# A graph network on one core: 16 of 2048 gathered rows of each body move from POOL's gather to single-row transfers of SP, empty edge tiles are skipped, and the setup is ordered anew

## The chip, the cores and the metric

One Trainium2 chip, one core. The metric is the device time of one launch in microseconds (us), the median of several runs. Less is better.

## The reference

Two graph-network layers over 6250 nodes with 160 features and 200,000 edges that are sorted by destination. Cut to what matters:

```
for layer in (0, 1):
    h   = node_features @ W_in * attr                 # a table of 6250 rows of 160 floats (640 B)
    w   = silu(edge_inputs @ fc1) @ fc2               # weights of each edge
    msg = w * h[edge_src] * edge_attr                 # one table row is gathered for each edge
    agg = segment_sum(msg, edge_dst)                  # summed at the destination nodes
    node_features = f(node_features, agg @ W_out, attr)   # layer norm with a residual between and after
```

The source nodes are random, so the rows `h[edge_src]` are read one by one from a table in HBM.

## The kernel before

There are five phases, with a barrier between them: `setup_phase` (weights, the first table, a table of destination windows), `edge_phase` for layer 0, `layer0_nodes_phase` (node update and the second table), `edge_phase` for layer 1, and `layer1_nodes_phase`.

The edges are padded to 200,704 and cut in tiles of 128 (one edge on each partition). Four tiles make a group, four groups a body, and there are 98 bodies. In `edge_phase` each engine runs its own loop over the bodies:

- POOL issues one indirect gather for each tile (`gather`, L542): 128 rows of 640 B from the table to `rows[j]`, by the tile's column of indices. A group's gathers wait until the sums that read the same buffer in the body before are done (`sum_done`), and until the index tile has come (`index_in`).
- SP loads, for each half body, the next indices (L484), the edge inputs (L489) and the edge attributes (L493); in the first 50 bodies also a node tile (L500 and L501 in layer 0, L503 and L507 in layer 1). The index load of a half waits until the gathers that used the buffer have landed (L483). Its two loops, over pairs of bodies, stand at L517 and L522.
- TensorE makes the hidden layer (L587), the edge weights (L600) and the products with one-hot matches that sum the messages by destination (L607). For each group it first loads a value from SBUF into a register (L644) and then waits (L647).
- ScalarE applies silu and scales the matches (L571).
- VectorE multiplies weights with gathered rows (L800 to L808, behind a wait on `gathered[j]`) and adds the sums. It loads a value for each group too (L707).

The order of the work is written out by hand, and all waits are on semaphores. Semaphores of a DMA rise by 16 when it has landed.

Of the kernel before, what the change touches and what calls it, by code (L numbers as in the profile page):

```python
# [11 lines left out]
P = 128  # L12
# [15 lines left out]
TPG = 4  # L28
# [22 lines left out]
INDEX_BUFFERS = 4  # L51
assert BODIES % 2 == 0 and NT % 2 == 0 and INDEX_BUFFERS == 4
# [54 lines left out]
def setup_phase(nc, d, w, sums):  # L107
    with ExitStack() as ctx:
# [37 lines left out]
        low, grp, totalled, counted = (sem(n) for n in ("low", "grp", "totalled", "counted"))  # L146
# [23 lines left out]
        def _(sp):  # L170
# [17 lines left out]
            for name in OTHERS:  # L188
                sp.dma_start(w[name][:, :], d[name]).then_inc(weights_in, 16)
            sp.dma_start(dst_tile[:, :], d["dst_tile"]).then_inc(dtile_in, 16)  # L190
# [4 lines left out]
            for c in range(len(STORES) - 1):  # L195
                store(c)
                if STORES[c + 1] == 30:
                    sp.wait_ge(low, 2)
                    sp.dma_start(d["lo_dram"].rearrange("(p q) -> p q", q=GQ), lo_i[:, :]).then_inc(lo_out, 16)
                if STORES[c + 1] == 40:  # L200
                    sp.wait_ge(lo_out, 16)
                    sp.dma_start(lo_all[:, :], d["lo_dram"].rearrange("(a g) -> a g", a=1).broadcast_to([P, G])).then_inc(lo_in, 16)
                    sp.wait_ge(grp, 12)
# [72 lines left out]
        def _(pe):  # L276
# [34 lines left out]
            for k in range(NT):  # L311
                project(k)
                if k == 35:
                    count_extras()
                if k == 41:
                    centre()
# [4 lines left out]
        def _(dve):  # L321
# [10 lines left out]
            def lowest():  # L332
                dve.wait_ge(dst_in, 16)
                nc.vector.tensor_reduce(lo_f[:, :], dst_by_group[:, :, :], mybir.AxisListType.X, ALU.min).then_inc(low, 1)

            def lowest_kept():
                dve.wait_ge(low, 1)
                nc.vector.tensor_scalar(lo_i[:, :], lo_f[:, :], float(NPAD - 1), None, ALU.min).then_inc(low, 1)

            def highest():  # L340
                nc.vector.tensor_reduce(hi_f[:, :], dst_by_group[:, :, :], mybir.AxisListType.X, ALU.max).then_inc(grp, 1)

            def spans():
                dve.wait_ge(grp, 1)
                nc.vector.scalar_tensor_tensor(out=span_f[:, :], in0=hi_f[:, :], scalar=float(NPAD - 1), in1=lo_f[:, :],
                                               op0=ALU.min, op1=ALU.subtract).then_inc(grp, 1)
                dve.wait_ge(grp, 2)
                nc.vector.tensor_scalar(span_i[:, :], span_f[:, :], 0.0, None, ALU.max).then_inc(grp, 1)

            def extras():  # L350
                dve.wait_ge(grp, 3)
                nc.vector.tensor_scalar(span_i[:, :], span_i[:, :], 3, None, ALU.arith_shift_right).then_inc(grp, 1)
                dve.wait_ge(grp, 4)
                nc.vector.tensor_scalar(span_i[:, :], span_i[:, :], 205, None, ALU.mult).then_inc(grp, 1)
                dve.wait_ge(grp, 5)
                nc.vector.tensor_scalar(entries[:, :, 1], span_i[:, :], 10, None, ALU.arith_shift_right).then_inc(grp, 1)

            def totals():
                dve.wait_ge(grp, 6)
                nc.vector.tensor_copy(extra_f[:, :], entries[:, :, 1]).then_inc(grp, 1)  # L360
                dve.wait_ge(low, 2)
                nc.vector.scalar_tensor_tensor(out=entries[:, :, 0], in0=lo_i[:, :], scalar=float(1 << EXTRA_BITS),
                                               in1=entries[:, :, 1], op0=ALU.mult, op1=ALU.add)
                dve.wait_ge(grp, 7)
# [4 lines left out]
            def partial(q):  # L369
                dve.wait_ge(grp, 8 + q)  # L370
                nc.vector.tensor_tensor(part_sum[:, q + 1:q + 2], part_sum[:, q:q + 1], extra_f[:, q:q + 1], ALU.add).then_inc(grp, 1)

            def table_entries():
                dve.wait_ge(grp, 11)
# [20 lines left out]
            for k in range(NT):  # L395
# [3 lines left out]
                if k == 13:  # L399
                    lowest()  # L400
                if k == 17:
                    highest()
                if k == 25:
                    lowest_kept()
                if k == 27:
                    spans()
                if k == 29:
                    extras()
                if k == 31:
                    totals()  # L410
                if k in (33, 34, 35):
                    partial(k - 33)
                if k == 38:
                    table_entries()
                if k == 45:
# [5 lines left out]
            relative()  # L421
# [3 lines left out]
def edge_phase(nc, d, w, sums, nodes, layer):  # L425
# [3 lines left out]
    with ExitStack() as ctx:  # L429
# [32 lines left out]
        prepared, zeroed = sem("prepared"), sem("zeroed")  # L462
# [8 lines left out]
        sum_done, added = sem("sum_done"), sem("added")  # L471
        x_rel, x_tile, x_matched, x_sum_done, x_added = (sem(n) for n in ("x_rel", "x_tile", "x_matched", "x_sum_done", "x_added"))
# [5 lines left out]
        def _(sp):  # L478
            def load(i, q, k):
                later = not (isinstance(i, int) and i == 0)  # L480
                if later:
                    for j in (2 * q, 2 * q + 1):
                        sp.wait_ge(gathered[j], GATHERED * i)  # L483
# [24 lines left out]
            def body(i, parity, with_base):  # L508
                for q in range(2):
                    load(i, q, (2 * parity + q + 2) % INDEX_BUFFERS)  # L510
                if with_base:
                    load_base(i)
                if with_base and L == 1 and not (isinstance(i, int) and i == 0):
                    store_self(i - 1)
# [757 lines left out]
```

## Time and profile before

| | |
|---|---|
| median of 3 runs | 4147.22 us (4146.08 to 4151.31) |
| profiled execution, own time | 4158.72 us |
| its span | 4157.0 us |
| POOL busy | 3019.7 us (73%) |
| PE (TensorE matmul) busy | 3299.3 us (79%) |
| ACT (ScalarE) busy | 2898.8 us (70%) |
| DVE (VectorE) busy | 2369.4 us (57%) |
| granted TensorE clock, mean | 0.988 |

The busy share is an average over the phases. SP issues DMAs and runs register instructions only; none of these count as busy, so the table has no row for it. An engine's sequencer, which runs such instructions, is written with a q (SPq, DVEq, PEldq).

### The profile page before, as it was taken

The page shows a single profiled execution, that of the slowest core. Times are in us where ns is not written, and L with a number is a line of the kernel's source. Part 1 is how long each engine was busy: PE and PEld are TensorE (multiplying, and loading weights), DVE is VectorE, ACT ScalarE, POOL GpSimd, SP SyncE. Part 2 cuts the span into 40 slices and gives each one's busy share as a digit, 9 for nine tenths or more (in the row PEclk, how much of TensorE's full clock was granted, in tenths as well). Part 3 has the DMA queues.
Part 4 walks back from the last instruction along what each step waited for, and adds up shares of the span by engine and source line. Part 5 has one row for each costly group of instructions (what it writes and reads, how often), then busy time and mean ns, then how long its engine had stood idle before and what let it go on. Part 6 is the DMA issues. An engine that isn't in the chain of part 4 may idle for free. (4 is left out here: it accounts for less than half of the span.)

```text
span 4157.0 us, 230556 instructions
## 1 busy us (share of the span) xinstructions
PE 3299.3 (79%) x91130; PEld 2543.6 (61%) x91131; DVE 2369.4 (57%) x6461; ACT 2898.8 (70%) x12105; POOL 3019.7 (73%) x3206
## 2 busy tenths in 40 slices
PE   7788888888777777777888888888878777777776
PEld 6666666666555555555766666666656565655656
DVE  5555555555444444444556666666666666666666
ACT  6666666666666666666477777777778777777776
POOL 5777777777777777777457777777777777777771
PEclk9999999999999999999999999999999999999998
DMA  5333333333222222222243434434333333333333
GB/s 154 83 83 82 85 82 83 82 82 85 73 72 73 72 73 72 72 73 72 77 131 105 107 104 107 107 104 107 104 105 98 93 94 96 93 96 94 93 96 107
DMA packets 361825, 382.01 MB, mean 92 GB/s; under 512 B 173617, under 2 KB 282997, under 8 KB 361662
## 3 DMA queue, kind: packets, MB, share of 16 engines
q0 software_dynamic: 150528, 257.10, 24.2%
q1 hardware_dynamic: 209936, 122.14, 10.4%
q10 hardware_dynamic: 1296, 1.91, 0.2%
q8 instruction: 39, 0.64, 0.1%
q14 instruction: 26, 0.21, 0.0%
HBM read 357.10 MB, written 23.76 MB: 92 GB/s over the span
## 5 line engine op out<-in xcount | busy, mean ns | idle before, releaser
L542 POOL DMA_INDIRECT e_rows<-scratch_table,k_index x3136 | 2972.7, 948 | 997.4 <-issue 900.6
L571 ACT ACTIVATE e_match<-e_match,e_attr 128x40 f32<-128x40 f32 x10976 | 2476.7, 316 | 0.0
L607 PE MATMUL e_sum<-e_match,e_msg 128*32 128x40 f32 (+1 forms) x81536 | 1438.0, 215 | 707.1 <-DVE e_msg L805 362.5
L607 PEld LDWEIGHTS e_sum<-e_match,e_msg 128*32 128x32 f32 x81536 | 1294.1, 111 | 1024.4 <-DVE e_msg L808 396.7
L800 DVE TENSOR_TENSOR e_msg<-e_w,e_rows 128x512 f32<-128x512 f32 x784 | 542.2, 692 | 1681.8 <-DMA e_rows<-scratch_table,k_index 1643.4
L564 ACT ACTIVATE e_hidden<-e_h 100x512 f32<-100x512 f32 (+1 forms) x784 | 384.7, 491 | 1138.0 <-PE e_h L587 1134.7
L600 PE MATMUL e_w<-k_fc,e_hidden 100*128 100x192 f32 (+1 forms) x6272 | 1025.5, 365 | 1.0 <-issue 1.0
L600 PEld LDWEIGHTS e_w<-k_fc,e_hidden 100*128 100x128 f32 (+1 forms) x6272 | 807.2, 189 | 348.1 <-issue 330.4
L587 PE MATMUL e_h<-e_inputs,k_fc 128*100 128x512 f32 (+1 forms) x1568 | 708.7, 534 | 116.6 <-issue 59.3
L803 DVE TENSOR_TENSOR e_msg<-e_w,e_rows 128x384 f32<-128x384 f32 x784 | 429.0, 547 | 0.0
L805 DVE TENSOR_TENSOR e_msg<-e_w,e_rows 128x384 f32<-128x384 f32 x784 | 429.0, 547 | 0.0
L587 PEld LDWEIGHTS e_h<-e_inputs,k_fc 128*100 128x100 f32 (+1 forms) x1568 | 216.7, 177 | 200.5 <-issue 152.0
L702 DVE TENSOR_TENSOR e_match<-e_misc,k_dst_rel 128x160 f32<-128x160 f32 x788 | 248.8, 316 | 2.1 <-issue 0.7
L736 DVE TENSOR_TENSOR sums<-sums,e_sum 128x160 f32 x784 | 242.9, 310 | 9.3 <-PE e_sum L607 8.5
L807 DVE TENSOR_TENSOR e_msg<-e_w,e_rows 128x384 f32<-128x384 f32 x392 | 214.2, 547 | 0.0
L808 DVE TENSOR_TENSOR e_msg<-e_w,e_rows 128x384 f32<-128x384 f32 x392 | 213.9, 546 | 0.0
L791 DVE TENSOR_TENSOR e_match<-e_misc,e_match 128x160 f32<-128x160 f32 x392 | 123.6, 315 | 0.0
L779 DVE COPY e_e_kept<-e_attr 128x48 f32<-128x48 f32 x392 | 81.7, 209 | 6.5 <-issue 3.6
L865 POOL MEMSET sums<- 128x512 f32 (+1 forms) x50 | 26.4, 528 | 59.1 <-PE m_agg L937 59.1
L903 ACT ACTIVATE m_yT<-m_tr 128x256 f32<-128x256 f32 x50 | 19.2, 386 | 47.9 <-PE m_tr L944 47.9
L778 DVE COPY e_misc<-e_attr 128x48 f32<-128x48 f32 x196 | 40.5, 207 | 10.3 <-DMA e_attr<-in_edge_attr 1.2
L1066 ACT ACTIVATE f_post<-f_pre 128x64 f32<-128x64 f32 x50 | 12.4, 248 | 31.4 <-DVE f_pre L1100 31.4
(130 smaller groups left out, 1032.7 us busy)
## 6 DMA issues: line engine op xcount, KB each, us to landing
e_rows<-scratch_table,k_index POOLq DMA_INDIRECT x3136
e_inputs<-in_inputs SPq DMA_DIRECT2D x196, 256.0 KB
e_attr<-in_edge_attr SPq DMA_DIRECT2D x392, 24.0 KB
e_inputs<-in_inputs SPq DMA_DIRECT2D x196, 40.0 KB
e_xb<-in_xT SPq DMA_DIRECT2D x50, 128.0 KB
scratch_yT<-m_yT SPq DMA_DIRECT2D x10, 640.0 KB, 4.6
e_xb<-scratch_yT SPq DMA_DIRECT2D x50, 128.0 KB
k_index<-in_src SPq DMA_DIRECT2D x396, 4.0 KB, 5.4
```

The source lines that it names most:

```text
L542: pool.indirect_dma_start(out=rows[j][:, t, :], out_offset=None, in_=table_dram, in_offset=bass.IndirectOffsetOnAxis(ap=index[k][:, c:c + ...
L564: nc.scalar.activation(hidden[j % 2][:, :], ps_h[0:layer.hid, 0:layer.group_cols], ACT.Silu, scale=layer.silu_scale).then_inc(silu_done, 1)
L571: last = nc.scalar.activation(match[j][:, t, c, :], match[j][:, t, 4, :], ACT.Copy, scale=attr[q][:, e0 + t, e:e + 1])
L587: nc.tensor.matmul(ps_h[0:layer.hid, 0:n], w[f"fc1_{L}"][:, :], inputs[j // 2][:, (j % 2) * n:(j % 2) * n + n], start=True, stop=True).the ...
L600: last = nc.tensor.matmul(ps_w[j % 2][:, c0:c0 + n], hidden[j % 2][k * h:k * h + k, u * P:(u + 1) * P], fc2[k * h:k * h + k, :], start=Tru ...
L607: return nc.tensor.matmul(out[32 * g:32 * g + 32, c0:c0 + n, :], m[:, f:f + 32], m5[:, which:which + n, :], start=first and opens, stop=en ...
L702: return nc.vector.tensor_tensor(into[:, :, 4, :], iota_t, rel_of(g).unsqueeze(2).broadcast_to([P, TPG, WIN]), ALU.is_equal)
L736: nc.vector.tensor_tensor(at, at, window, ALU.add).then_inc(added, 1)
L800: nc.vector.tensor_tensor(m[:, :, 0:128].rearrange("p t (k n) -> p t k n", k=2), wt[:, :, 0:128].rearrange("p t (k n) -> p t k n", k=2), r ...
L803: nc.vector.tensor_tensor(comps(m[:, :, 128:224]), w_v(128), comps(r[:, :, 64:160]), ALU.mult)
L805: last = nc.vector.tensor_tensor(comps(m[:, :, 224:320]), w_v(160), comps(r[:, :, 64:160]), ALU.mult)
L807: nc.vector.tensor_tensor(comps(m[:, :, 320:416]), w_v(192), comps(r[:, :, 64:160]), ALU.mult)
```

## The change

It has three parts.

1. The last tile of each body (group 3, tile 3) is gathered by POOL for partitions 0 to 111 only. SP fetches rows 112 to 127: for each it loads the index from SBUF into a register and issues a DMA of one row from the table into `sp_rows` (one of two buffers). Eight rows are fetched behind the first half's loads and eight at the body's end. In the next body, behind the first half's loads, SP copies the 16 rows with one DMA into the group's tile. VectorE's multiplies of group 3 wait for that copy too (`sp_copied`).
2. The padding, which stood at the end of the edge list, is now the first tiles of the first body: `EMPTY = (2, 1, 1, 1)` tiles of its four groups. They are cleared by VectorE and not gathered (five gathers fewer in each phase); waits on `gathered` change by as much.
3. The setup has another order: reductions of the destination table are made in four parts each and later, the first store of the table stands ahead of other loads, and `relative()`, which makes the relative destinations, stands at tile 41 where it stood at the end.

```diff
+EMPTY = (2, 1, 1, 1)
+BY_SP = 16
+BY_POOL = P - BY_SP
...
+            def copy_rows(i, parity):
+                landed, summed = 16 * BY_SP * i + 16 * BY_SP, GPB * i
+                if not isinstance(i, int):
+                    sp.compute_val(landed)
+                    sp.compute_val(summed)
+                sp.wait_ge(sp_landed, landed)
+                at_least(sp, sum_done, summed)
+                sp.dma_start(rows[GPB - 1][BY_POOL:P, TPG - 1, :], sp_rows[parity][BY_POOL:P, :]).then_inc(sp_copied, 16)
+
+            def fetch_rows(pair, parity, first, last):
+                i, k = 2 * pair + parity, 2 * parity + 1
+                if first == BY_POOL:
+                    if not isinstance(pair, int):
+                        used, copied = 32 * pair, 16 * i - 16
+                        sp.compute_val(used)
+                        sp.compute_val(copied)
+                        sp.wait_ge(prepared, 1)
+                        sp.wait_ge(index_in[k], used)
+                        sp.wait_ge(sp_copied, copied)
+                for p in range(first, last):
+                    row = sp.value_load(index[k][p:p + 1, STEP - 1:STEP], min_val=0, max_val=NPAD - 1)
+                    sp.dma_start(sp_rows[parity][p:p + 1, :], table_dram[bass.ds(row, 1), :]).then_inc(sp_landed, 16)
+
+            def body(pair, parity, with_base):
+                i, half = 2 * pair + parity, BY_POOL + BY_SP // 2
+                started = not (isinstance(i, int) and i == 0)
+                load(i, 0, (2 * parity + 2) % INDEX_BUFFERS)
+                if started:
+                    copy_rows(i - 1, 1 - parity)
+                fetch_rows(pair, parity, BY_POOL, half)
+                load(i, 1, (2 * parity + 3) % INDEX_BUFFERS)
+                if with_base:
+                    load_base(i)
+                if with_base and L == 1 and started:
+                    store_self(i - 1)
+                fetch_rows(pair, parity, half, P)
...
+                first = isinstance(count, int) and not parity
...
-                for t in range(TPG):
+                for t in range(EMPTY[j] if first else 0, TPG):
                     c = (j % 2) * TPG + t
+                    p = BY_POOL if (j, t) == (GPB - 1, TPG - 1) else P
                     pool.indirect_dma_start(
-                        out=rows[j][:, t, :], out_offset=None, in_=table_dram,
-                        in_offset=bass.IndirectOffsetOnAxis(ap=index[k][:, c:c + 1], axis=0),
+                        out=rows[j][0:p, t, :], out_offset=None, in_=table_dram,
+                        in_offset=bass.IndirectOffsetOnAxis(ap=index[k][0:p, c:c + 1], axis=0),
                     ).then_inc(gathered[j], 16)
...
-                dve.wait_ge(gathered[j], GATHERED * i + GATHERED)
+                dve.wait_ge(gathered[j], GATHERED * i + GATHERED - 16 * EMPTY[j])
+                if j == GPB - 1:
+                    dve.wait_ge(sp_copied, 16 * i + 16)
...
-                if k == 13:
-                    lowest()
-                if k == 17:
-                    highest()
+                if k in (24, 25, 26, 27):
+                    lowest(k - 24)
+                if k in (28, 29, 30, 31):
+                    highest(k - 28)
...
+                if k == 41:
+                    relative()
...
-            relative()
             dve.wait_ge(rel_made, 2)
```

SP's queue in layer 0's second loop, one body without node tile, before. `ISA` is a register instruction; L484, L489 and L493 are the three loads of a half body.

```order
L484 ISA
L484 DMA k_index<-in_src 128x8
L485 ISA
L489 ISA
L489 DMA e_inputs<-in_inputs 10x1024
L491 REGISTER_ALU
L493 ISA
L493 DMA e_attr<-in_edge_attr 128x48
L484 ISA
L484 DMA k_index<-in_src 128x8
L489 ISA
L489 DMA e_inputs<-in_inputs 10x1024
```

The same place now, from the attribute load of the first half on (L506 is what L493 was). L528 is the copy of the 16 rows of the body before, L535 the head of `fetch_rows`, and L541 and L542 are a row's value load and its address and DMA.

```order
L506 DMA e_attr<-in_edge_attr 128x48
L524 ISA
L528 DMA e_rows<-e_sp_rows 16x160
L535 ISA
L541 TENSOR_LOAD k_index
L541 ISA x2
L542 ISA
L542 DMA e_sp_rows<-scratch_table 1x160
L541 TENSOR_LOAD k_index
L541 ISA x2
L542 ISA
L542 DMA e_sp_rows<-scratch_table 1x160
```

The four rows from L541 on stand eight times there, and eight times more behind the second half's loads.

## Rows read from the trace of the kernel before

**Rows 1.** The page's costliest groups: busy, mean ns of one, idle before with releasers.

```profile
L542 POOL DMA_INDIRECT e_rows<-scratch_table,k_index x3136 | 2972.7, 948 | 997.4 <-issue 900.6
...
L800 DVE TENSOR_TENSOR e_msg<-e_w,e_rows 128x512 f32<-128x512 f32 x784 | 542.2, 692 | 1681.8 <-DMA e_rows<-scratch_table,k_index 1643.4
```

**Rows 2.** POOL's timeline, one body of layer 0: start us, duration us.

```profile
1000.00 0.95 POOL L542 DMA_INDIRECT e_rows<-scratch_table,k_index  x1 [0.30 <-issue]
1001.25 0.94 POOL L542 DMA_INDIRECT e_rows<-scratch_table,k_index  x1 [0.30 <-issue]
...
1020.04 0.95 POOL L542 DMA_INDIRECT e_rows<-scratch_table,k_index  x1 [0.30 <-issue]
```

**Rows 3.** POOL's waits over the whole span: us in total, times, longest.

```profile
POOL e_rows L542 <- PE e_sum L607: 55.1, 181, 0.3
```

**Rows 4.** SP's timeline, a body without node tile: start us, duration us.

```profile
1987.45 0.35 SPq L484 DMA_DIRECT2D k_index<-in_src  x1
...
1988.72 0.34 SPq L493 DMA_DIRECT2D e_attr<-in_edge_attr  x1
...
1998.03 0.30 SPq L489 DMA_DIRECT2D e_inputs<-in_inputs  x1
1998.57 0.34 SPq L493 DMA_DIRECT2D e_attr<-in_edge_attr  x1
```

**Rows 5.** SP's line L483 in two short windows: ns min/median/max, first and last start.

```profile
L483 SPq EVENT_SEMAPHORE  x1: 17/17/17, 1987.2 to 1987.2; - x1
...
L483 SPq EVENT_SEMAPHORE  x1: 17/17/17, 1997.3 to 1997.3; - x1
```

**Rows 6.** SP's timeline, second half of a body with node tile.

```profile
1016.32 0.35 SPq L493 DMA_DIRECT2D e_attr<-in_edge_attr  x1
1016.90 0.35 SPq L500 DMA_DIRECT2D nodes<-in_x  x1
1017.45 0.33 SPq L501 DMA_DIRECT2D e_xb<-in_xT  x1
```

**Rows 7.** Line L517, the end of SP's loop over pairs.

```profile
L517 SPq FUSED_REGOPS  x48: 50/50/60, 76.1 to 3059.1; - x48
L517 SPq ALU_OP  x48: 37/37/37, 115.9 to 3098.9; - x48
L517 SPq COMPARE_BRANCH  x48: 40/45/59, 115.9 to 3099.0; - x48
```

**Rows 8.** TensorE's value load L644 and the instruction behind it, window 1003.5 to 1004.6.

```profile
L644 PEldq FUSED_REGOPS  x2: 55/103/151, 1003.7 to 1004.2; - x2
L644 PEldq TENSOR_LOAD <-k_table x1: 302/302/302, 1003.8 to 1003.8; - x1
L644 PEldq SEQ_ASSERT  x1: 18/18/18, 1004.4 to 1004.4; - x1
...
L647 PEldq EVENT_SEMAPHORE  x1: 51/51/51, 1004.5 to 1004.5; - x1
```

**Rows 9.** Value loads of TensorE (L644) and VectorE (L707), all of them.

```profile
L644 PEldq TENSOR_LOAD <-k_table x784: 296/300/488, 61.0 to 4083.6; - x196
...
L707 DVEq TENSOR_LOAD <-k_table x784: 302/306/552, 64.4 to 4083.2; - x196
```

**Rows 10.** Line L501: SP's register instructions ahead of a DMA with a computed address.

```profile
L501 SPq FUSED_REGOPS  x48: 42/43/43, 95.4 to 1037.4; - x48
L501 SPq MOVE e_xb<-in_xT x48: 29/29/29, 95.4 to 1037.5; - x48
```

**Rows 11.** Line L207: SP's one DMA that has a single partition (1x1568).

```profile
L207 SPq DMA_DIRECT2D k_table<-scratch_tab_dram x1: 242/242/242, 47.4 to 47.4; - x1
```

**Rows 12.** Timeline, end of setup and start of layer 0's edge phase.

```profile
48.02 1.78 DVE L387 SCALAR_TENSOR_TENSOR k_dst_rel<-dst_tile_i,lo_all 128x1568 f32<-128x1568 int32 x1
...
51.49 1.10 POOL L542 DMA_INDIRECT e_rows<-scratch_table,k_index  x1 [30.05 <-POOLq L108]
...
62.23 0.69 DVE L800 TENSOR_TENSOR e_msg<-e_w,e_rows 128x512 f32<-128x512 f32 x1 [6.22 <-PE e_w L600]
```

**Rows 13.** SP's waits over the whole span.

```profile
SPq L211 <- DMA scratch_table<-h: 1.1, 1, 1.1
```

**Rows 14.** Timeline: the first attribute load, and VectorE released by it.

```profile
53.39 0.36 SPq L493 DMA_DIRECT2D e_attr<-in_edge_attr  x1
...
55.25 0.21 DVE L778 COPY e_misc<-e_attr 128x48 f32<-128x48 f32 x1 [1.21 <-DMA e_attr<-in_edge_attr]
```

More of the change, by code:

```diff
@@ L51 @@
 INDEX_BUFFERS = 4
+EMPTY = (2, 1, 1, 1)
+BY_SP = 16
+BY_POOL = P - BY_SP
+assert 0 <= EPAD - EDGES - sum(EMPTY) * P <= (TPG - EMPTY[0]) * P
 assert BODIES % 2 == 0 and NT % 2 == 0 and INDEX_BUFFERS == 4
@@ L189, in _ @@
                 sp.dma_start(w[name][:, :], d[name]).then_inc(weights_in, 16)
+            store(0)
             sp.dma_start(dst_tile[:, :], d["dst_tile"]).then_inc(dtile_in, 16)
@@ L471, in edge_phase @@
         sum_done, added = sem("sum_done"), sem("added")
+        sp_rows = [sb(f"sp_rows{b}", [P, D]) for b in range(2)]
+        sp_landed, sp_copied = sem("sp_landed"), sem("sp_copied")
         x_rel, x_tile, x_matched, x_sum_done, x_added = (sem(n) for n in ("x_rel", "x_tile", "x_matched", "x_sum_done", "x_added"))
@@ L481, in load @@
                 if later:
+                    landed = [GATHERED * i - 16 * EMPTY[j] for j in (2 * q, 2 * q + 1)]
+                    if not isinstance(i, int):
+                        for value in landed:
+                            sp.compute_val(value)
                     for j in (2 * q, 2 * q + 1):
-                        sp.wait_ge(gathered[j], GATHERED * i)
+                        sp.wait_ge(gathered[j], landed[j - 2 * q])
                     sp.dma_start(index[k][:, :], d["src"][:, bass.ds((2 * i + q + 2) * STEP, STEP)]).then_inc(index_in[k], 32)
@@ L507, in store_self @@
                 sp.dma_start(d["self1"][bass.ds(i * P, P), :], self_t[:, :]).then_inc(self_out, 16)
-            def body(i, parity, with_base):
-                for q in range(2):
-                    load(i, q, (2 * parity + q + 2) % INDEX_BUFFERS)
+            def copy_rows(i, parity):
+                landed, summed = 16 * BY_SP * i + 16 * BY_SP, GPB * i
+                if not isinstance(i, int):
+                    sp.compute_val(landed)
[3 more added lines that the diff above has]
+                sp.dma_start(rows[GPB - 1][BY_POOL:P, TPG - 1, :], sp_rows[parity][BY_POOL:P, :]).then_inc(sp_copied, 16)
@@ L523, in _ @@
                 for parity in range(2):
-                    body(2 * pair + parity, parity, False)
+                    body(pair, parity, False)
+            copy_rows(BODIES - 1, 1)
             for k in range(2):
@@ L810, in messages @@
                 return window_at
+            for j in range(GPB):
+                nc.vector.memset(rows[j][:, 0:EMPTY[j], :], 0.0).then_inc(cleared, 1)
             for g in range(AHEAD):
@@ L1215, in lay_out, with in_slots @@
     r["attr"] = by_partition(padded(np.concatenate([a["node_vec1"], a["node_vec1_n2"], a["node_vec1_n3"]], 1), NPAD))
-    r["src"] = by_partition(padded(a["src"], EPAD + 2 * STEP * P))
-    dst = padded(a["dst"], EPAD, NODES)
+    slot = np.full(EPAD, -1)
+    free = np.ones(EPAD, bool)
+    for g in range(GPB):
+        free[g * GE:g * GE + EMPTY[g] * P] = False
+    free[EMPTY[0] * P:EPAD - EDGES - sum(EMPTY[1:]) * P] = False
+    slot[free] = np.arange(EDGES)
+    following = np.minimum.accumulate(np.where(slot < 0, EDGES, slot)[::-1])[::-1]
+    def in_slots(v):
+        return np.where((slot >= 0).reshape((-1,) + (1,) * (v.ndim - 1)), v[following], 0).astype(v.dtype)
+    r["src"] = by_partition(padded(in_slots(a["src"]), EPAD + 2 * STEP * P))
+    dst = a["dst"][following]
     r["dst_tile"] = by_partition(dst)
     r["dst_by_group"] = dst.reshape(GP, GQ, GE)
-    e = padded(a["edge_attr_4"], EPAD)
+    e = in_slots(a["edge_attr_4"])
     r["edge_attr"] = by_partition(np.concatenate([e, e[:, 1:3]], 1))
-    r["inputs0"] = padded(a["edge_attr_10"], EPAD).T.copy()
-    r["inputs1"] = padded(a["edge_attr_64"], EPAD).reshape(G, 2, 2, P, NB1).transpose(1, 4, 0, 2, 3).reshape(2 * NB1, EPAD // 2)
+    r["inputs0"] = in_slots(a["edge_attr_10"]).T.copy()
+    r["inputs1"] = in_slots(a["edge_attr_64"]).reshape(G, 2, 2, P, NB1).transpose(1, 4, 0, 2, 3).reshape(2 * NB1, EPAD // 2)
     L0 = {k[7:]: v for k, v in a.items() if k.startswith("L0_gnn_")}
```

70 lines of the change are left out of this document (36 added, 34 removed).

## The prediction

> **What bounds the kernel now.** I read the page's costliest groups first, since they give each engine's busy time with what ended its idle time [rows 1]: POOL issues 3136 gathers, busy 2972.7 us, and its idle time of 997.4 us is nearly all "issue", a gap that belongs to the instruction. VectorE's first multiply of a group (L800) is idle 1681.8 us before it, 1643.4 of them for the gathered rows. So rows are what is late, and POOL makes them. POOL's timeline shows how regular that is [rows 2]: 16 gathers, one body, from 1000.00 to 1020.04, so 20.04 us a body and 1.2525 us a gather (0.95 busy, 0.30 gap). The waits of POOL [rows 3] show that TensorE's sums, which free the row buffers, cost it 55.1 us over 181 times, 0.30 each: the same gap, not a wait. Both edge phases have 98 bodies, 196 x 20.04 = 3928 us of a span of 4157.0.
>
> Then SP, which is to get new work. It has nothing busy in the page, but its timeline shows its queue [rows 4, 5]. In a body without node tile it passes the first wait (L483) at 1987.2 and ends its third DMA at 1989.06; it passes the second at 1997.3 and ends at 1998.91. That is 1.86 + 1.61 us of work, with 8.2 us of waiting between. The two loads of a node tile (bodies 0 to 49 of each phase) add 1.1 us: the DMA before them starts at 1016.32 and ends at 1016.67, the last ends at 1017.78 [rows 6]. The loop's end costs some 0.3 us for two bodies (three short instructions of 37 to 50 ns and their gaps) [rows 7]. SP thus works 3.6 or 4.7 us of 20.04; some 15 to 16 us are free. The change asks for them.
>
> **The change: 16 rows a body on SP.** Each row is a value load (a load, a fused register instruction, an assert), an address instruction and a DMA of one row, as the order shows. No SP value load is in the trace, but TensorE's has the same three instructions: load starts at 1003.8, assert at 1004.4, the next instruction (L647) at 1004.5 [rows 8], so 0.6 to 0.7 us, of which the load records 0.30 and the fused instruction 0.15. VectorE's loads take 0.306, so this duration hardly depends on the engine [rows 9]. SP's gaps between short instructions are smaller than TensorE's (its wait instruction takes 17 ns [rows 5] and TensorE's 51 [rows 8]); I take 0.61. From below it is 0.30 + 0.15 + 0.02 and three gaps of 0.03: 0.56; from above 0.67, TensorE's own. The address: between the DMA of L500 (1016.90 + 0.35) and that of L501 (1017.45) lie 0.20 us, which hold a fused instruction of 43 ns, a move of 29 ns and gaps [rows 6, 10]; I take 0.19. The DMA itself: the one transfer with a single partition took SP 0.242 us [rows 11], against 0.30 to 0.35 of the wider ones [rows 4]; I take 0.24, bounds 0.22 and 0.30. Sum: 0.61 + 0.19 + 0.24 = 1.04 us a row (bounds 0.97 and 1.10), and 16.6 us for 16 rows.
>
> **The copy and the waits.** The copy of 16 rows into the group's tile is one more DMA of 0.35 us, a register instruction and two waits with gaps: 0.5. The head of the row fetch (one register instruction, three waits): 0.2. In the other loads the new wait values go into register instructions that are there already: 0.
>
> **SP's body.** Without node tile 1.86 + 1.66 (with the gap behind) + 0.15 + 0.5 + 0.2 + 16.6 = 21.0 us; with it 22.1 us. Both are over POOL's 20.04. SP then never waits, and it is the bound, because every loop closes through it: POOL's index tiles, TensorE's inputs and the attributes are its loads, and VectorE's last group of each body now also waits for its copy. Behind a row fetch stand, in SP's queue, the second half's loads; they come 8.3 us later in the body, still within a period. The other loops are shorter than 21 us: from the sum that frees a row buffer to the next sum of the same buffer it is four gathers (5.0), landing, multiplies and products, some 13 us. Per phase 48 bodies lose 21.0 - 20.04 = 0.96 and 50 lose 2.06, in both phases 92 + 206 = 298 us.
>
> **The other parts.** Five gathers fewer in each phase are 10 x 1.2525 = 12.5 us of POOL. They move POOL ahead at a phase's start only; with SP as the bound they are worth 0. The gather of 112 rows: the trace has only 128. Between 0 (all fixed) and an eighth of 0.95, 0.12 us, less; here hidden under SP, 0 again. The clears of the five tiles (VectorE) lie in its wait of 6.22 us before the first L800 [rows 12]. Setup: taking the 1.78 us instruction L387 from VectorE's end to k = 41 frees little, since the release waits for the last table store: SP's wait at L211 is 1.1 us, and VectorE had ended at 49.80 with POOL's first gather at 51.49 [rows 12, 13]. In its new place it delays the last stores by what VectorE can't absorb. Splitting the reductions moves work, it adds some small gaps. I take 0, bounds -3 and +3.
>
> **The sum.** Profiled execution 4158.7 + 298 = 4457; the median of the three times is 4147.2, 11.5 lower, so 4445 us, 7.2% over before.
>
> **Rivals.**
> 1. *SP keeps up, POOL stays the bound: faster.* It needs a row at 0.90 us or less (5.5 + 14.4 = 19.9). For it: SP's short instructions are quicker than TensorE's, and the row DMA has no equal in the trace. Against: load, fused instruction and DMA alone record 0.30 + 0.15 + 0.24 = 0.69; assert, address and move (0.09) and six gaps then have 0.21, so 0.02 a gap, where SP's three between L500 and L501 have (0.20 - 0.07) / 3 = 0.04 each. Gain: 12.5 for the empty tiles, up to 196 x 0.12 = 23 for the narrower gather: 4112 (4108 to 4135). Chance 0.14. It decides at about 0.92 us a row over all bodies: there what the bodies with node tile lose is what the others win.
> 2. *SP binds mostly in the bodies with node tile.* A row at 0.93 to 0.97: 4165 to 4290. Chance 0.09.
> 3. *The copy waits for its rows.* Between the last row's issue and the copy's wait lie about 0.3 + 1.9 = 2.2 us; the first attribute load, issued at 53.39, had released VectorE at 55.25, 1.86 us later [rows 14]. Landings 1 us later would cost 196 x 0.8 = 157 us: about 4600, and more if they queue. The Trainium skill, "DMA: Bandwidth & Descriptors", section "Why a DMA increments its semaphore by 16 and not by 1", has one-partition transfers from SP all on the one lowest engine; the trace names no engines, so nothing here shows it, and it would speak for this rival. Chance 0.06.
> 4. *The load itself is twice as long on SP.* Records of 0.60 for 0.30 give 1.34 a row, bodies of 25.8 and 26.9, and 557 + 690 = 1247 us: 5394. Against it are TensorE's and VectorE's nearly equal 0.30. The Trainium skill, same page, section "Latency and other measured facts", gives a load to a register a floor of about 600 ns; the rows have 0.30 for the instruction and 0.6 from its start to its assert, so the trace agrees only if the figure means the latter. Chance 0.03.
>
> **How the numbers follow.** My forecast has 0.68: with the row at 0.98 to 1.10, 4300 to 4630. The range leaves out rival 1 (0.14) and rival 4 with the worst of rival 3 (0.05), and reaches from rival 2's start to a row at 1.10 with a copy that waits 0.5: 4160 to 4690. A measurement of this kernel tells about 0.2% (8 us). Faster 0.14, same 0.03, slower 0.83.
>
> **What would show it.** Right: SP has hardly a wait left in the edge phases; POOL's gaps grow and are released by sums or by the index load; L800's wait for the last group of a body is for the copy; bodies of about 21 and 22 us, the first half of a phase slower than the second. A row's pitch on SP is read between two of its DMAs (1.04). Wrong: SP still waits for gathered rows each half body, and POOL's pitch is unbroken. That happens if SP's value load is much under 0.6 us. The 112-row gather shows its own duration either way.

## The result and the profile after

| | before | this kernel |
|---|---|---|
| median (6 runs each) | 4147.18 us | 5303.53 us |
| lowest to highest | 4146.08 to 4151.31 | 5274.97 to 5310.06 |
| profiled execution, own time / span | 4158.72 / 4157.0 | 5276.04 / 5274.3 |
| granted TensorE clock, mean | 0.988 | 0.842 |

The ratio over all runs is 1.2769 (1.2751 to 1.2787; the two medians alone give 1.2788): 28% slower. The forecast was 4445 us. The direction came out as forecast, and so did the bound, SP; the size didn't: SP costs 5.8 us a body over POOL's 20.04, where 1.5 was forecast.

Page of the kernel after: its first line, two lines of the 40 slices (POOL's digit is its busy time in tenths of a slice, and it is 5 or 6 nearly everywhere, so the loss is spread over both edge phases; PEclk is the granted TensorE clock in tenths of full speed), and four of the costliest groups, with idle time and its releaser, which answer to [rows 1].

```profile
span 5274.3 us, 250541 instructions
...
POOL 5555555555565565656445555555555656565652
PEclk8888888888888888888988888888888888888878
...
L587 POOL DMA_INDIRECT e_rows<-scratch_table,k_index x3126 | 2953.5, 945 | 2127.0 <-PE e_sum L652 1253.0
...
L632 PE MATMUL e_h<-e_inputs,k_fc 128*100 128x512 f32 (+1 forms) x1568 | 868.5, 642 | 1404.9 <-DMA e_inputs<-in_inputs 1390.2
L849 DVE TENSOR_TENSOR e_msg<-e_w,e_rows 128x512 f32<-128x512 f32 x784 | 542.0, 691 | 2334.3 <-PE e_w L645 2324.1
L609 ACT ACTIVATE e_hidden<-e_h 100x512 f32<-100x512 f32 (+1 forms) x784 | 384.1, 490 | 2277.1 <-PE e_h L632 2273.2
```

Read it backwards from POOL. The gathers take as long as before, but 2127.0 us of idle time stand ahead of them instead of 997.4, most of it for TensorE's sums. The multiply L849 (L800 before) no longer waits for gathered rows but for edge weights (L645), and the first matmul of the hidden layer (L632) waits for `e_inputs`, a load of SP. TensorE ties the two together: its program order is the hidden layer of a group, the edge weights of the group before, and the sums of the group before that, so that all three stand behind one load. The timeline shows it once (start us, duration us; in brackets the idle time before and what ended it).

```profile
1303.13 1.14 PE L632 MATMUL e_h<-e_inputs,k_fc 128*100 128x512 f32 x2 [3.94 <-DMA e_inputs<-in_inputs]
...
1304.06 2.77 PE L645 MATMUL e_w<-k_fc,e_hidden 100*128 100x192 f32 x8
...
1304.30 0.60 ACT L609 ACTIVATE e_hidden<-e_h 100x512 f32<-100x512 f32 x1 [4.53 <-PE e_h L632]
...
1306.76 1.62 PE L652 MATMUL e_sum<-e_match,e_msg 128*32 128x120 f32 x80
1306.93 0.69 DVE L849 TENSOR_TENSOR e_msg<-e_w,e_rows 128x512 f32<-128x512 f32 x1 [6.14 <-PE e_w L645]
...
1309.26 0.95 POOL L587 DMA_INDIRECT e_rows<-scratch_table,k_index  x1 [3.36 <-PE e_sum L652]
```

The weights at 1304.06 start before ScalarE's activation at 1304.30, and the sums at 1306.76 before the multiply at 1306.93: what held both was TensorE's own order, not the data of this group. The gather at 1309.26 follows the sums.

SP's waits, before and after (us in total, times, longest). Before:

```profile
SPq L483 <- DMA e_rows<-scratch_table,k_index: 1638.5, 209, 9.5
```

After; L528 is the copy's wait:

```profile
SPq L497 <- DMA e_rows<-scratch_table,k_index: 3.1, 12, 0.7
...
SPq L528 <- DMA e_sp_rows<-scratch_table: 1.4, 2, 0.7
```

SP has hardly a wait left in the edge phases, so it is the bound. Its timeline shows the second half of a body with node tile and the first half of the next (start us, duration us; a row with x8 runs from the start of the first to the end of the last):

```profile
1301.02 0.29 SPq L502 DMA_DIRECT2D e_inputs<-in_inputs  x1
1301.56 0.36 SPq L506 DMA_DIRECT2D e_attr<-in_edge_attr  x1
...
1304.02 9.08 SPq L542 DMA_DIRECT2D e_sp_rows<-scratch_table  x8
1313.87 0.39 SPq L497 DMA_DIRECT2D k_index<-in_src  x1
...
1315.17 0.36 SPq L506 DMA_DIRECT2D e_attr<-in_edge_attr  x1
1315.73 0.55 SPq L528 DMA_DIRECT2D e_rows<-e_sp_rows  x1
1317.53 9.06 SPq L542 DMA_DIRECT2D e_sp_rows<-scratch_table  x8
```

Eight rows hold seven pitches: (9.08 - 0.26) / 7 = 1.26 us a row, where 1.04 was forecast and 1.10 was the upper bound. Copies follow one another at 26.4 us where there is a node tile and at 25.2 without one, in both layers (forecast 22.1 and 21.0). 100 bodies lose 6.3 us and 96 lose 5.2, together 1129; with the 4147 of before that is 5276, the time of the profiled execution. (Four of the six runs took 27 to 34 us more than that one; their mean granted clock was 0.835 or 0.836, that of the other two 0.842 and 0.839. None of the four has a profile, and their surplus stays open.)

SP's lines of one row (ns min/median/max, first and last start):

```profile
L541 SPq TENSOR_LOAD <-k_index x3136: 467/499/736, 52.1 to 5194.2; - x196
L541 SPq FUSED_REGOPS  x3136: 152/152/192, 52.6 to 5194.8; - x196
L541 SPq SEQ_ASSERT  x3136: 18/18/33, 52.8 to 5195.0; - x196
...
L542 SPq FUSED_REGOPS  x3136: 37/37/48, 52.9 to 5195.0; - x196
L542 SPq MOVE e_sp_rows<-scratch_table x3136: 29/38/125, 53.0 to 5195.1; - x196
L542 SPq DMA_DIRECT2D e_sp_rows<-scratch_table x3136: 154/260/310, 53.1 to 5195.2; - x196
```

The medians sum to 1.00 us, so 0.25 is gaps, as assumed. One record stands out: the load takes 0.50, not the 0.30 that it takes on TensorE and VectorE [rows 9].

### The profile page after: what moved, and what is told of

Same layout as the page of the kernel before. It is cut to its first block and busy times, and to the rows that moved or that the text cites. A ratio compares the mean times of both kernels' runs of the same rounds, so it can differ in the third digit from the quotient of the medians.

```text
span 5274.3 us, 250541 instructions
## 1 busy us (share of the span) xinstructions
PE 3834.3 (73%) x91130; PEld 2944.9 (56%) x91131; DVE 2492.1 (47%) x6475; ACT 2897.4 (55%) x12105; POOL 3000.5 (57%) x3196
## 5 line engine op out<-in xcount | busy, mean ns | idle before, releaser
L587 POOL DMA_INDIRECT e_rows<-scratch_table,k_index x3126 | 2953.5, 945 | 2127.0 <-PE e_sum L652 1253.0
L632 PE MATMUL e_h<-e_inputs,k_fc 128*100 128x512 f32 (+1 forms) x1568 | 868.5, 642 | 1404.9 <-DMA e_inputs<-in_inputs 1390.2
L849 DVE TENSOR_TENSOR e_msg<-e_w,e_rows 128x512 f32<-128x512 f32 x784 | 542.0, 691 | 2334.3 <-PE e_w L645 2324.1
L652 PEld LDWEIGHTS e_sum<-e_match,e_msg 128*32 128x32 f32 x81536 | 1427.8, 122 | 325.6 <-issue 300.4
L652 PE MATMUL e_sum<-e_match,e_msg 128*32 128x40 f32 (+1 forms) x81536 | 1550.3, 230 | 4.3 <-issue 3.5
L645 PE MATMUL e_w<-k_fc,e_hidden 100*128 100x192 f32 (+1 forms) x6272 | 1343.0, 453 | 0.5 <-issue 0.5
L645 PEld LDWEIGHTS e_w<-k_fc,e_hidden 100*128 100x128 f32 (+1 forms) x6272 | 1045.3, 239 | 467.9 <-issue 431.3
L632 PEld LDWEIGHTS e_h<-e_inputs,k_fc 128*100 128x100 f32 (+1 forms) x1568 | 252.4, 205 | 1495.3 <-issue 1456.5
L916 POOL MEMSET sums<- 128x512 f32 (+1 forms) x50 | 26.4, 527 | 60.7 <-PE m_agg L988 60.7
L1017 DVE SCALAR_TENSOR_TENSOR nodes<-m_agg,k_masked,nodes 128x160 f32<-128x160 f32 x50 | 19.2, 384 | 23.8 <-PE m_agg L988 23.0
```

Source lines behind the costliest of these rows:

```text
L587: pool.indirect_dma_start(out=rows[j][0:p, t, :], out_offset=None, in_=table_dram, in_offset=bass.IndirectOffsetOnAxis(ap=index[k][0:p, c: ...
L632: nc.tensor.matmul(ps_h[0:layer.hid, 0:n], w[f"fc1_{L}"][:, :], inputs[j // 2][:, (j % 2) * n:(j % 2) * n + n], start=True, stop=True).the ...
L645: last = nc.tensor.matmul(ps_w[j % 2][:, c0:c0 + n], hidden[j % 2][k * h:k * h + k, u * P:(u + 1) * P], fc2[k * h:k * h + k, :], start=Tru ...
L652: return nc.tensor.matmul(out[32 * g:32 * g + 32, c0:c0 + n, :], m[:, f:f + 32], m5[:, which:which + n, :], start=first and opens, stop=en ...
L849: nc.vector.tensor_tensor(m[:, :, 0:128].rearrange("p t (k n) -> p t k n", k=2), wt[:, :, 0:128].rearrange("p t (k n) -> p t k n", k=2), r ...
```

## The experiments

In all, the time is device time, each run is one kernel that was executed 2 to 11 times, the ratio is to the kernel before on the same chip (medians 4147.5, 4148.3 and 4149.5 in the three batches). Diffs are against this kernel unless said otherwise.

### First batch: the parts without SP's rows

**e1_rest.** Empty tiles and new setup alone; POOL gathers all 128 rows and SP fetches none.

```diff
                 load(i, 0, (2 * parity + 2) % INDEX_BUFFERS)
-                if started:
-                    copy_rows(i - 1, 1 - parity)
-                fetch_rows(pair, parity, BY_POOL, half)
                 load(i, 1, (2 * parity + 3) % INDEX_BUFFERS)
...
-                fetch_rows(pair, parity, half, P)
...
-                    p = BY_POOL if (j, t) == (GPB - 1, TPG - 1) else P
+                    p = P
...
-                if j == GPB - 1:
-                    dve.wait_ge(sp_copied, 16 * i + 16)
```

> The changed kernel without its first part: POOL gathers all 128 rows of the last tile and SP fetches none, so that only the empty tiles and the new setup are left. Theory A (all of the loss is SP's row work, the rest is harmless): ten gathers fewer at 1.2525 us are 12.5 us, and in the changed kernel's trace POOL's first gather starts at 49.8 instead of 51.5 us, 1.7 us; so about 14 us under before, near 4133 us. Rival B (something in the rest costs too, such as VectorE's extra waits in every group or the moved padding): at or over 4147 us.

Measured: 4139.72 us (4135.18 to 4141.80), ratio 0.9981 (0.9972 to 0.9990): 7.8 us gained where 14 were expected. So all of the loss belongs to the change's first part, the 16 rows, and the rest is a small gain.

**e2_empty.** The kernel before with the empty tiles alone: e1_rest with the old `setup_phase`.

```diff
-                for t in range(TPG):
+                for t in range(EMPTY[j] if first else 0, TPG):
```

> Before with the empty tiles alone, its own setup kept. Theory A: POOL is the bound and starts five gathers ahead in each phase, 12.5 us, near 4134.7 us. Rival: the head start is given back, because in the second body POOL waits for the first body's sums, which the first edge weights hold back anyway: then near 4147, and the gain of the full rest is the setup's.

Measured: 4140.24 us, ratio 0.9979 (0.9970 to 0.9988), so 7.3 us gained where ten gathers make 12.5. POOL's timeline at the start of both phases, and its waits, show where the missing 5 can have gone:

```profile
66.28 0.94 POOL L579 DMA_INDIRECT e_rows<-scratch_table,k_index  x1 [0.69 <-PE e_sum L644]
...
76.53 0.95 POOL L579 DMA_INDIRECT e_rows<-scratch_table,k_index  x1 [0.55 <-PE e_sum L644]
...
2152.38 0.94 POOL L579 DMA_INDIRECT e_rows<-scratch_table,k_index  x1 [3.12 <-PE e_sum L644]
...
POOL e_rows L579 <- PE e_sum L644: 97.7, 298, 3.1
```

At 0.30 a gap, 298 gaps are 89.4 us; 8.3 are real waits, where before it was 55.1 - 181 x 0.30 = 0.8 [rows 3]. POOL comes earlier to buffers that TensorE still reads. That is 7.5 us more, even somewhat over the missing 5; it comes from two single profiles, and the rest stays open.

**e3_setup.** The kernel before with the new `setup_phase` alone.

```diff
-                if k == 13:
-                    lowest()
-                if k == 17:
-                    highest()
+                if k in (24, 25, 26, 27):
+                    lowest(k - 24)
+                if k in (28, 29, 30, 31):
+                    highest(k - 28)
...
+                if k == 41:
+                    relative()
...
-            relative()
```

> Before with the new setup alone. Theory A: the first gather starts 1.7 us earlier, near 4145.5 us. My prediction had 0 with bounds of 3 us on both sides. Rival: within 0.5 us of before, the 1.7 us being chance of one profile.

Measured: 4147.84 us, ratio 1.0000 (0.9991 to 1.0009). In the single profiles the first gather starts at 49.83 instead of 51.49 us, but the times don't show it: within 0.5 us of before, as the rival had it.

**e4_pool112.** e1_rest, with POOL's gather of 112 rows in the last tile. Rows 112 to 127 of that buffer are filled once a phase, with rows that the reference doesn't take.

```diff
+            sp.dma_start(rows[GPB - 1][112:P, TPG - 1, :], table_dram[0:P - 112, :]).then_inc(filled, 16)
...
                 if isinstance(i, int):
                     dve.wait_ge(cleared, GPB)
+                    dve.wait_ge(filled, 16)
```

> As the first kernel of this call (empty tiles and new setup), but POOL gathers only 112 rows in the last tile of each body. Rows 112 to 127 of that tile are left out: they are filled once a phase with the table's first rows, and SP fetches nothing after that. Theory A: a gather's cost is nearly fixed; single gathers of 112 rows in the changed kernel's trace take 0.93 us against 0.94 to 0.95, so 196 x 0.015 is 3 us under the first kernel of this call. Rival C, the upper bound of my prediction: an eighth of 0.95, 196 x 0.12 is 23 us under it.

Measured: 4139.38 us, ratio 0.9979 (0.9970 to 0.9988), as e1_rest. Two gathers in a row, the second with 112 rows:

```profile
1001.59 0.94 POOL L583 DMA_INDIRECT e_rows<-scratch_table,k_index  x1 [0.30 <-issue]
1002.84 0.92 POOL L583 DMA_INDIRECT e_rows<-scratch_table,k_index  x1 [0.30 <-issue]
```

An eighth fewer rows makes a gather 0.02 us shorter, not 0.12: its cost is nearly all fixed. 196 x 0.02 = 4 us at most, and that doesn't show. The 23 us of the rival don't exist. What SP took over was worth nothing to POOL.

### Second batch: why a row takes 1.26 us

Open was why the load takes 0.50: a load on SP is slow in itself (S), it is slow behind a transfer (Q), or it depends on the partition it reads from, 112 and up (P).

**s1_loads.** Sixteen loads a body stay, the sixteen transfers go; one transfer of the last row to all 16 partitions takes their place, so 15 rows are not those of the reference.

```diff
-                landed, summed = 16 * BY_SP * i + 16 * BY_SP, GPB * i
+                landed, summed = 16 * i + 16, GPB * i
...
-                    sp.dma_start(sp_rows[parity][p:p + 1, :], table_dram[bass.ds(row, 1), :]).then_inc(sp_landed, 16)
+                if first != BY_POOL:
+                    sp.dma_start(sp_rows[parity][BY_POOL:P, :], table_dram[bass.ds(row, 1), :].broadcast_to([BY_SP, D])).then_inc(sp_landed, 16)
```

> The changed kernel with its 16 value loads a body, but without their 16 row transfers: one transfer a body brings 16 copies of one row, so the other 15 rows of the tile are left out. In the changed kernel a row takes SP 1.25 us, of it 0.50 for the load's own record, where TensorE's and VectorE's loads take 0.30. Theory S (a load simply takes SP 0.50): loads still record 0.50, 0.80 us from load to load, SP has about 19.5 us of work a body with node tile and POOL is the bound again or nearly so, 4135 to 4180 us. Theory Q (a load waits for the transfer that SP issued just ahead of it): behind another load it records 0.30, 0.60 from load to load, and SP waits 3 us a body more.

Measured: 4139.00 us, ratio 0.9977 (0.9966 to 0.9989). The load's line over the whole span, and then over one block of eight:

```profile
L541 SPq TENSOR_LOAD <-k_index x3136: 267/274/749, 51.2 to 4046.7; - x196
...
L541 SPq TENSOR_LOAD <-k_index x8: 274/275/473, 1306.3 to 1310.4; - x8
```

A load takes 0.27 us, except one of each eight, with 0.47 here: the first, which has the attribute load's DMA ahead of it. In the body's other block of eight the first stands behind the copy, with the head of `fetch_rows` between, and takes 0.56. Sixteen loads still fit under POOL.

**s2_transfers.** The sixteen transfers stay, from constant rows; the loads go.

```diff
-                    row = sp.value_load(index[k][p:p + 1, STEP - 1:STEP], min_val=0, max_val=NPAD - 1)
-                    sp.dma_start(sp_rows[parity][p:p + 1, :], table_dram[bass.ds(row, 1), :]).then_inc(sp_landed, 16)
+                    sp.dma_start(sp_rows[parity][p:p + 1, :], table_dram[p:p + 1, :]).then_inc(sp_landed, 16)
```

> The changed kernel with the 16 row transfers but without the value loads: the rows' addresses are constants, so the rows brought are not the edge's. Both theories: 0.26 us and a gap, 0.31 us a row, 5 us a body, SP at about 11 us of 20; POOL is the bound, near 4140 us as the rest alone. If instead the transfers or their landing were the cost (my third rival: they queue, the copy waits for them), it stays well over 4200 us.

Measured: 4139.42 us, ratio 0.9979 (0.9968 to 0.9991). A line and a stretch of the timeline:

```profile
L541 SPq DMA_DIRECT2D e_sp_rows<-scratch_table x3136: 162/252/438, 52.3 to 4043.1; - x196
...
1318.61 2.36 SPq L541 DMA_DIRECT2D e_sp_rows<-scratch_table  x8
```

That is (2.36 - 0.25) / 7 = 0.30 us a transfer. Neither half of a row's work alone is slow, and neither alone takes SP over POOL's 20.04 us a body, the threshold from which SP is the bound.

**s3_grouped.** All of the work, with the eight loads ahead of the eight transfers.

```diff
-                for p in range(first, last):
-                    row = sp.value_load(index[k][p:p + 1, STEP - 1:STEP], min_val=0, max_val=NPAD - 1)
+                loaded = [sp.value_load(index[k][p:p + 1, STEP - 1:STEP], min_val=0, max_val=NPAD - 1) for p in range(first, last)]
+                for p, row in zip(range(first, last), loaded):
                     sp.dma_start(sp_rows[parity][p:p + 1, :], table_dram[bass.ds(row, 1), :]).then_inc(sp_landed, 16)
```

> The changed kernel with eight value loads first and their eight transfers after, the work being the same. Theory S: loads record 0.50, a body stays at 26.4 us, 5300 us within 30. Theory Q: seven of eight loads record 0.30, a body is 16 x 0.875 x 0.2 = 2.8 us shorter, near 4750 us.

Measured: 4489.39 us (4488.45 to 4490.33), ratio 1.0823 (1.0792 to 1.0855): 814 us less for another order of the same instructions. Lines and timeline:

```profile
L540 SPq TENSOR_LOAD <-k_index x3136: 267/274/726, 52.4 to 4402.9; - x196
...
L540 SPq TENSOR_LOAD <-k_index x8: 273/274/469, 1302.3 to 1306.4; - x8
...
L542 SPq DMA_DIRECT2D e_sp_rows<-scratch_table x3136: 207/228/315, 57.3 to 4406.6; - x196
...
1307.11 3.14 SPq L542 DMA_DIRECT2D e_sp_rows<-scratch_table  x8
```

The loads are at 0.27 again. Of the seven pitches in 4.1 us the first is 0.20 longer, so the others are (4.1 - 0.2) / 7 = 0.56; a transfer with its address is (3.14 - 0.23) / 7 = 0.42. With an eighth of those 0.20 a row is then 1.0 us, where it was 1.26; copies follow one another at 22.35 and 21.15 us, 4.1 less than in this kernel. S falls: the same load on the same engine is at 0.27. Q gave the direction, but the run is some 260 us better than the 4750 that Q expected: the loads account for 3.1 us of the 4.1 (14 of them 0.225 shorter), the shorter transfers (0.228 for 0.260) for 0.5, and the gaps for the rest. Why those shrank is open.

**s4_partition0.** The loads read partitions 0 to 15 (other rows than the reference's).

```diff
-                    row = sp.value_load(index[k][p:p + 1, STEP - 1:STEP], min_val=0, max_val=NPAD - 1)
+                    row = sp.value_load(index[k][p - BY_POOL:p - BY_POOL + 1, STEP - 1:STEP], min_val=0, max_val=NPAD - 1)
```

> The changed kernel, but SP's loads read the indices of partitions 0 to 15 instead of 112 to 127 (so it fetches other edges' rows). TensorE's and VectorE's loads of 0.30 read partition 0. Theory P (the partition matters): loads record 0.30, a body is 3.2 us shorter, near 4680 us. Theories S and Q: 0.50 and 5300 us within 30.

Measured: 5253.01 us, ratio 1.2664 (1.2627 to 1.2701).

```profile
L541 SPq TENSOR_LOAD <-k_index x3136: 458/493/721, 50.9 to 5171.7; - x196
```

The load stays at 0.49. P, which expected 4680, falls. The two executions are 17 us under the range of S and Q; loads that are 0.006 us shorter make 19 of the 24 us between the two profiled executions, and the rest stays open.

So the load is slow behind a transfer and quick behind another load. On SP no run has a load with neither just ahead of it, so "behind a transfer" and "not behind a load" aren't told apart there; TensorE's and VectorE's loads at 0.30 [rows 9] come once a group, with neither ahead, but on other engines.

### Third batch: the threshold

SP's body is 16 rows plus 5.07 us (6.26 with a node tile); it crosses POOL's 20.04 at a row of 0.94 (0.86). Four kernels go from the row of 1.26 towards and under that.

**f2_nocheck.** Loads still behind transfers, without the range check of each index (a fused instruction of 0.15 and an assert).

```diff
-                    row = sp.value_load(index[k][p:p + 1, STEP - 1:STEP], min_val=0, max_val=NPAD - 1)
+                    row = nc.s_assert_within(sp.value_load(index[k][p:p + 1, STEP - 1:STEP]), 0, NPAD - 1,
+                                             skip_runtime_bounds_check_because="indices are below NPAD")
```

> The changed kernel without the range check of the value loads, each load still right behind a transfer. Theory T with loads that stay at 0.50 behind a transfer: 1.256 - 0.25 is 1.00 us a row, bodies of 22.3 and 21.2 us, 4150 + 100 x 2.25 + 96 x 1.1 is about 4480 us. Rival: without the check's instructions the load's latency shows in the address instruction instead and the row stays at 1.1 us or more: 4630 us or over.

Measured: 4390.28 us, ratio 1.0583 (1.0562 to 1.0604).

```profile
L541 SPq TENSOR_LOAD <-k_index x3136: 441/504/727, 51.3 to 4309.5; - x196
...
L543 SPq DMA_DIRECT2D e_sp_rows<-scratch_table x3136: 254/263/305, 52.0 to 4310.2; - x196
...
1317.41 7.14 SPq L543 DMA_DIRECT2D e_sp_rows<-scratch_table  x8
```

A row is (7.14 - 0.26) / 7 = 0.98, so the check costs 0.27, more than its two records (0.17). Copies follow one another at 21.85 and 20.65 us, where 22.3 and 21.2 were expected, so the run is 90 us under the 4480 of theory T; the rival's 4630 falls. The load stays at 0.50: the check, which stood between the load and the row's own transfer, isn't what makes it slow.

**f1_grouped_nocheck.** s3_grouped and f2_nocheck in one, all parts of the change and the whole computation.

```diff
+                loaded = [nc.s_assert_within(sp.value_load(index[k][p:p + 1, STEP - 1:STEP]), 0, NPAD - 1,
+                                             skip_runtime_bounds_check_because="indices are below NPAD")
+                          for p in range(first, last)]
+                for p, row in zip(range(first, last), loaded):
```

> All three parts of the change kept, 16 rows on SP, but eight value loads stand together ahead of their eight transfers, and the loads have no range check (a fused instruction and an assert, 0.25 us with gaps). Theory T (SP's work per body against POOL's 20.04 us decides, and nothing else of the change costs): the row falls from 1.00 us (grouped) to 0.75, SP's body with node tile from 22.3 to 18.3 us, SP waits for POOL again, and the time is that of the rest alone, 4139 us within 6. Rival K (the copy that group 3 waits for, or the row transfers' traffic, costs by itself): over 4160 us. Rival G (the narrower gather gains once SP keeps up): 4116 us.

Measured: 4143.53 us (4140.78 to 4146.31), ratio 0.9987 (0.9977 to 0.9996). Waits and SP's line:

```profile
L540 SPq TENSOR_LOAD <-k_index x3136: 267/275/729, 52.0 to 4049.4; - x196
...
L540 SPq TENSOR_LOAD <-k_index x8: 273/277/466, 1307.7 to 1310.0; - x8
...
SPq L496 <- DMA e_rows<-scratch_table,k_index: 270.0, 208, 2.3
...
POOL e_rows L589 <- PE e_sum L654: 89.1, 257, 3.2
```

SP waits for gathered rows again, so POOL is the bound, at 20.0 us a body. That is theory T; K (over 4160) and G (4116) fall. From load to load it is now (2.3 - 0.19) / 7 = 0.30 us. All of the 28% is gone, but the kernel isn't better than e1_rest (4139.7, in another batch; the intervals of the ratios overlap).

**f3_rows12.** This kernel with 12 rows a body by SP (rows 112 to 123). The last four are filled once a phase and are not the reference's.

```diff
-BY_SP = 16
-BY_POOL = P - BY_SP
+BY_SP = 12
+BY_POOL = 112
+TOP = BY_POOL + BY_SP
```

> The changed kernel with SP fetching 12 rows a body (partitions 112 to 123) at 1.256 us each; rows 124 to 127 are left out (filled once a phase). Theory T: 15.1 + 6.25 is 21.3 us with node tile and 20.1 without, against 20.0 of POOL: 4140 + 100 x 1.3 + 96 x 0.15, about 4285 us. Rival: a body's length is set by a loop of waits through SP's late loads, and falls less than 1.256 us a row: over 4400 us.

Measured: 4341.20 us, ratio 1.0465 (1.0444 to 1.0486).

```profile
1307.98 0.81 SPq L530 DMA_DIRECT2D e_rows<-e_sp_rows  x1
1310.08 6.58 SPq L544 DMA_DIRECT2D e_sp_rows<-scratch_table  x6
```

The row's pitch is unchanged, (6.58 - 0.26) / 5 = 1.26. What was not foreseen is the copy: 12 rows took 0.81 us, 16 rows 0.55. With it, 100 bodies of 21.5 and 96 of 20.4 us give 4147 + 146 + 35 = 4328; the run is 13 above that and 56 above the expected 4285. The rival's 4400 falls.

**f4_rows8.** The same with eight rows (120 to 127 left out in the same way).

```diff
-BY_SP = 16
-BY_POOL = P - BY_SP
+BY_SP = 8
+BY_POOL = 112
+TOP = BY_POOL + BY_SP
```

> The same with 8 rows (partitions 112 to 119), rows 120 to 127 left out. Theory T: 10.0 + 6.25 is 16.3 us, under POOL's 20.0, so 4139 us within 6, and no gain from the 8 rows that SP does fetch. Rival G: under 4125 us.

Measured: 4140.07 us, ratio 0.9979 (0.9968 to 0.9989).

```profile
SPq L497 <- DMA e_rows<-scratch_table,k_index: 445.0, 219, 3.3
...
L530 SPq DMA_DIRECT2D e_rows<-e_sp_rows x196: 677/688/773, 64.8 to 4048.9; - x196
```

Under the threshold, and at the time of e1_rest: eight rows by SP cost nothing and bring nothing. Their copy took 0.69 us, so its time doesn't grow with the rows: 0.69 for 8, 0.81 for 12, 0.55 for 16.

## Why the size was wrong

By the prediction's steps:

- **What bounds the kernel:** right. POOL's 20.04 us a body held until SP's own body crossed it; f1, f4, s1 and s2 end at 4139 to 4144.
- **"SP then never waits, and it is the bound":** right. 1638.5 us of waits for gathered rows became 3.1. The chain that closes through SP was `e_inputs` to TensorE, whose hidden layer, weights and sums stand in one queue, and then POOL. I had named index tiles, inputs and attributes together, and it was the inputs that came last. L849's wait for the copy, which I had said would show in the last group of a body, ended only 3 of its waits, 4.2 us in all; for the rest the edge weights were later (687 waits, 2324.1 us).
- **"1.04 us a row (bounds 0.97 and 1.10)":** this step failed, in its term "0.61" for the value load. I took its 0.30 from TensorE's and VectorE's loads, with the argument that the duration hardly depends on the engine. That is so (s1: 0.27 on SP), but neither of those engines loads right behind a DMA that it has issued itself, and here each load does. The load took 0.50 instead of 0.30, the transfer 0.26 instead of 0.24, and gaps were as assumed: 0.22 x 16 = 3.5 us a body, 196 x 3.5 = 690 us. For the value load the bounds held only the gaps open, not the load's own record, so they were too narrow. s1, s3, s4 and f2 show the cause as far as it goes: a load behind a transfer is slow, on partitions 0 to 15 as on 112 to 127, with or without a check, and one behind a load is not.
- **The bounds' own sum:** the upper ends of the terms, 0.67 + 0.19 + 0.30, make 1.16 and not 1.10; the DMA's 0.30 was dropped. Even 1.16 gives only about 4820 us. In the range, a row at 1.10 with a copy that waits 0.5 is 4633 + 98, about 4730 and not 4690. Neither slip decides anything.
- **"The copy: 0.5", "the other loads: 0":** too small. From the attribute load's end to the copy's end it is 1316.28 - 1315.53 = 0.75 us, with 0.55 for the DMA itself where I took 0.35 from the wide transfers; the 0.5 for the whole copy is 0.25 short. SP's work other than rows is 5.1 and 6.3 us where the sum had 4.4 and 5.5, so 0.7 more; the other 0.45 lies in the new register instructions and their gaps, which I haven't split further. 196 x 0.7 = 140 us.
- Together, from the forecast of the profiled execution: 4457 + 690 + 140 = 5287, within 11 us of its 5276. Above the threshold each tenth of a microsecond in a row costs 196 x 1.6 = 314 us. So much leverage wanted a range that reached up further.
- **Empty tiles, setup, narrow gather "worth 0" here:** right. Where POOL is the bound they are worth 7.3 us, nothing, and nothing that shows.
- **Rival 1 (SP keeps up):** false. Even f1, with a row well under its threshold, reached 4143.5 and not 4112: I had given the narrower gather up to 23 us, and it has none.
- **Rival 2 (SP binds mostly with a node tile):** false here; at the row of 1.26 SP binds in every body.
- **Rival 3 (the copy waits for its rows):** false, with 1.4 us of waits for `e_sp_rows` in the whole span; the copy is issued too late to wait for anything. The counts of the queue whose bytes grew, before and after, show that a row was not spread over several engines either: 12,544 more packets are two for each of the 3136 rows fetched and 3136 rows copied. Which engine took them isn't shown.

```profile
q1 hardware_dynamic: 209936, 122.14, 10.4%
...
q1 hardware_dynamic: 222480, 126.18, 9.1%
```

- **Rival 4 (the load twice as long on SP, 5394):** nearest in its time, but not the mechanism. It made a property of the engine of what is a property of the order, and s3 refutes that too. The Trainium skill, "DMA: Bandwidth & Descriptors", section "Latency and other measured facts", has a floor of about 600 ns for such a load and says that the compiler unrolls four times to amortize it. The traces have 0.27 and 0.50 for the record and 0.30 from load to load in f1, so the figure is not borne out for loads behind loads. What unrolling would save isn't in the page; here eight loads put together made a row 0.26 us shorter (s3).

Not settled: why a load takes some 0.2 us more behind a transfer that its own queue has issued. Nor was it tried to take a whole tile's gather from POOL; only the empty tiles show what gathers that go whole are worth.

The best versions that compute the whole are the empty tiles with or without the new setup, 4140 us, 0.2% under the kernel before. Which of them is better can't be told.

## What to carry to other kernels

Before work goes to an idle queue, ask what the busy engine saves: a gather of 112 rows costs POOL 0.92 us and one of 128 rows 0.94, so moving 16 of 128 rows wasn't worth it at any price on the other side (smaller gathers weren't measured). A sequencer's free time is a threshold: eight rows cost nothing, twelve cost 4.7%, sixteen 28%. Take an instruction's duration from rows where it stands behind the same neighbour, and put loads in front together, with the transfers that use them after.

## What the runs showed of the hardware

- A value load on SP takes 0.27 us behind another load, 0.47 to 0.50 behind a DMA that SP has issued, the attribute load in s1 or a row transfer in this kernel, and 0.56 in the one place read behind the copy (s1). Single-row transfers take 0.23 us side by side with computed addresses (s3), 0.25 with constant ones (s2) and 0.26 between value loads.
- A range check on a loaded value costs 0.27 us of the sequencer's time (f2), though its records are 0.17.
- A copy from SBUF to SBUF took SP 0.69 us for 8 rows (f4), 0.81 for 12 (f3) and 0.55 for 16 (this kernel).
- The mean granted clock was lower in the runs where TensorE had to wait: 0.988 before, 0.911 in s3, 0.842 in this kernel. In the half body shown, TensorE was idle for 3.9 us up to 1303.1; the granted clock was 1.00 up to 1304.0, 0.50 (1.2 GHz) from 1304.1 to 1306.7, and 1.00 (2.4 GHz) again from 1308.4 on. Eight weight products (L645) took 2.77 us at the lower level and 1.47 at the higher one, from 1296.36 on. With SP as the bound that lies off the path.
